# The head of a pre-layernorm transformer layer in another order: early weights, VectorE low halves, second x ahead of the feed-forward's weights, dummy transposes

## What is computed

```python
x = x + attn(layernorm(x))      # causal, ALiBi bias per head, softmax, Wo and bo
x = x + ffn(layernorm(x))       # sigmoid(x1) * x2, weights quantised to -1, 0, 1
# attn: q, k, v = n @ W + b; scores = q k^T / 4 + slope_h * distance; softmax; @ v; @ Wo + bo
# ffn:  w -> clip(round(w / (mean|w| + 1e-8)), -1, 1); hidden = sigmoid(x @ w1.T) * (x @ w2.T); hidden @ w3.T
```

## Time and profile before

| | us |
|---|---|
| median of 3 runs | 677.22 (677.1 to 678.31) |
| the profiled execution, its own time | 679.13 |
| its span on the core | 677.3 |
| PE busy | 617.9 (91%) |
| DVE busy | 463.4 (68%) |
| ACT busy | 366.2 (54%) |
| POOL busy | 118.3 (17%) |
| DMA, moved in all | 57.64 MB, mean 85 GB/s |

### The profile page before, as it was taken

One profiled execution on the slowest core, in us unless ns is written; L12 is line 12 of the kernel. 1 busy time (PEld: TensorE's weight loads), 2 busy tenths in 40 slices (PEclk: granted clock), 3 DMA queues, 4 the chain that ended last, 5 costly groups with the idle time before them and its releaser, 6 DMA issues.

```text
span 677.3 us, 10966 instructions
## 1 busy us (share of the span) xinstructions
PE 617.9 (91%) x3710; PEld 378.2 (56%) x3710; DVE 463.4 (68%) x1189; ACT 366.2 (54%) x770; POOL 118.3 (17%) x146
## 2 busy tenths in 40 slices
PE   1787888889999989999999999899999999999997
PEld 1444555546565646455556575555555555565486
DVE  4357878666776967568787778778788787511075
ACT  2424454564554435647655535467677675576521
POOL 5464300031021220320001212003100000132100
PEclk9959998899999979999999999899999999999999
DMA  8664664555131313543231131136332120011000
GB/s 249 168 176 117 163 145 111 132 171 144 33 80 34 95 32 81 174 128 81 64 69 45 33 88 41 48 80 131 95 97 49 39 76 0 2 42 42 1 17 31
DMA packets 26635, 57.64 MB, mean 85 GB/s; under 512 B 4756, under 2 KB 14484, under 8 KB 22996
## 3 DMA queue, kind: packets, MB, share of 16 engines
q1 hardware_dynamic: 26580, 56.95, 32.8%
HBM read 41.87 MB, written 14.80 MB: 84 GB/s over the span
## 4 chain that ended last, share of the span: by engine, by line
PE 78%; DVE 9%; ACT 4%; issue 4%; DMA 3%; SPq 1%; POOL 0%; ACTq 0%; POOLq 0%
PE pS L940 20%; PE pO L953 19%; PE pM L920 18%; PE pM L895 5%; PE pM L841 3%; PE pM L904 3%; DVE pm L1092 2%; PE pS L943 2%; DVE pM L1095 2%; PE pM L881 2%; PE pS L904 1%; PE pM L847 1%; ACT probs L785 1%; DMA qst<-mT 1%; PE pS L841 1%
## 5 line engine op out<-in xcount | busy, mean ns | idle before, releaser
L785 ACT ACTIVATE probs<-pS 128x512 f32<-128x512 f32 (+3 forms) x640 | 308.5, 545 | 247.0 <-PE pS L943 122.0
L1092 DVE TENSOR_REDUCE pm<-pM 128x1 f32<-128x512 f32 x384 | 240.4, 681 | 64.2 <-PE pM L920 63.2
L920 PE MATMUL pM<-kst,qst 126*128 126x512 f32 (+3 forms) x640 | 240.3, 404 | 22.0 <-ACT qk_hl L742 6.0
L940 PE MATMUL pS<-qst,kst 128*128 128x512 f32 (+3 forms) x640 | 249.7, 406 | 6.6 <-DMA qst<-mT 4.4
L940 PEld LDWEIGHTS pS<-qst,kst 128*128 128x128 f32 x640 | 121.5, 192 | 88.7 <-issue 57.4
L1095 DVE CUSTOM_DVE_ANT_0 pM<-pM,mask 128x128 f32<-128x128 f32 (+3 forms) x256 | 119.3, 517 | 66.0 <-PE pM L920 65.6
L920 PEld LDWEIGHTS pM<-kst,qst 126*128 126x128 f32 x640 | 122.8, 198 | 51.5 <-ACT qk_hl L742 7.0
L953 PE MATMUL pO<-probs,vals 128*17 128x512 f32 (+3 forms) x1280 | 134.9, 540 | 0.0
L953 PEld LDWEIGHTS pO<-probs,vals 128*17 128x17 f32 x1280 | 29.6, 97 | 65.7 <-issue 40.9
L943 PE MATMUL pS<-maskb,identb 128*128 128x128 bf16 x256 | 59.0, 233 | 0.0
L642 POOL TENSOR_TENSOR rstd<-ve,mhalf 128x4 f32<-128x4 f32 (+1 forms) x9 | 8.5, 945 | 219.5 <-DVE ve L1008 219.4
(11 more groups left out here) (145 smaller groups left out, 418.8 us busy)
## 6 DMA issues: line engine op xcount, KB each, us to landing
kst<-parts SPq DMA_DIRECT2D x40, 512.0 KB
parts<-qk_hl SPq DMA_DIRECT2D x32, 256.0 KB, 3.1
qst<-parts SPq DMA_DIRECT2D x32, 256.0 KB, 4.5
ctx_dram<-ctx_raw SPq DMA_DIRECT2D x15, 256.0 KB, 4.0
xin<-in_L_attn_x SPq DMA_DIRECT2D x5, 512.0 KB, 5.4
out<-work SPq DMA_DIRECT2D x8, 256.0 KB, 2.2
work<-ctx_dram SPq DMA_DIRECT2D x7, 256.0 KB
work<-rden_dram SPq DMA_DIRECT2D x7, 256.0 KB
```

Of the source, the lines that this page charges most:

```text
L785: nc.scalar.activation(probs[:, n % PSLOTS, q0:CH], pS[:, n % SBANKS, q0:CH], ACT.Exp)\
L920: pe.matmul(max_bank(x)[:, 0:N], qst[0:R_MAX, u % QSLOTS, h, t * P:(t + 1) * P], kst[0:R_MAX, n % KSLOTS, h, 0:N], start=True, stop=True). ...
L940: ins = pe.matmul(pS[:, n % SBANKS, q0:CH], kst[0:R_END, sl, h, b:b + P], qst[0:R_END, u % QSLOTS, h, q0:CH], start=True, stop=not is_diag ...
L1092: nc.vector.tensor_reduce(dst, bank, AX.X, ALU.max).then_inc(max_free, 1)
```

## The change

- **SP**: Wk and Wq come right behind x of chunk 0 and have a semaphore of their own (`wqk_in`), the biases of k and q too (`bias_in`). Then Wv and bv, x of chunk 1 and the table's parts, and only then w1 and w2. w3 comes behind the stores of k(0,1) and q(0,1), Wo and bo behind `load_q(1)`.
- **PE**: 30 transposes of the identity into itself (`WARM_UP`) run from the moment the identity is there; nobody reads them. The transposes of chunk 0 start tile by tile (`xn0_ok`). k(1,0) and q(1,0) run among the turns of unit 0, after its 4th and its 8th turn; k(1,1) and q(1,1) take their old place after `swap_max(0)`; v(1,0) and v(1,1) are now the groups of steps 0 and 1, and steps 2 and 3 have none.
- **ACT and DVE**: for k(0,0), q(0,0), k(0,1), q(0,1) ACT writes the high half only, and DVE makes the low half straight from PSUM (`split_head`). The factor of q goes into its weights. For all other k and q groups nothing changes, except that ACT applies no factor.
- **POOL**: the constants of the masks come behind the first layernorm, `key_rows(0)` and the zeros of `qst` ahead of it, the ones of `qst` behind it.
- **DVE**: layernorm of chunk 0 is first, the table second; the statistics of chunk 1 stand between `split_head` of q(0,0) and of k(0,1).

The core of the diff:

```diff
-            lst = lst[4:] + [None] * 3
+            lst = lst[6:] + [None] * 5
...
-    head_first, head_last = pre_groups(0) + pre_groups(1)[:2], [("gamma",)] + pre_groups(1)[2:4]
-    head_groups = head_first + head_last
+    head_first, head_last = pre_groups(0) + pre_groups(1)[:2], [("gamma",)] + pre_groups(1)[4:6]
+    head_between = {G - 1: ("k", 1, 0), 2 * G - 1: ("q", 1, 0)}
+    head_groups = head_first + list(head_between.values()) + head_last
+    head_splits = [g for g in head_first if g[0] in "kq"]
+    WARM_UP = 30
...
+        def need_split(eng, g):
+
+            if g in head_splits:
+                need_empty(eng, g)
+            else:
+                eng.wait_ge(split_ok, split_no[g] - len(head_splits) + 1)
...
             load_x(0)
+            for dst, src in ((w_raw[0], Wk), (w_raw[1], Wq)):
+                sp.dma_start(dst, src.rearrange("(k p) n -> p k n", p=P)).then_inc(wqk_in, 16)
             sp.dma_start(al[:, 0, :], alibi).then_inc(al_in, 16)
...
+            sp.dma_start(wv_s[:, :, :], Wv.rearrange("(k p) n -> p k n", p=P)).then_inc(w_in, 16)
+            sp.dma_start(bv_b[:, :], bv.rearrange("(a n) -> a n", a=1).to_broadcast([P, D])).then_inc(w_in, 16)
+            load_x(1)
+            sp.wait_ge(al_ok, 2)
...
-            sp.dma_start(w_rows[2], w3.rearrange("(t p) n -> p t n", p=P)).then_inc(raw_in, 16)
...
             store_parts(("k", 0, 1))
             store_parts(("q", 0, 1))
+            sp.dma_start(w_rows[2], w3.rearrange("(t p) n -> p t n", p=P)).then_inc(w3_in, 16)
             load_k(1)
             load_q(1)
+            sp.dma_start(wo_s[:, :, :], Wo.rearrange("(k p) n -> p k n", p=P)).then_inc(wo_in, 16)
+            sp.dma_start(bo_b[:, :], bo.rearrange("(a n) -> a n", a=1).to_broadcast([P, D])).then_inc(wo_in, 16)
+            store_parts(("k", 1, 0))
+            store_parts(("q", 1, 0))
             load_m(0)
...
+            key_rows(0)
+            query_zeros(0)
+            power(1)
+            pool.wait_ge(xn0_ok, TPC)
+            query_ones(0)
...
+            for g in head_first[:KT]:
+                side_op(g)
+            act.wait_ge(bias_in, 64)
...
+            for g in head_first[KT:KT + len(head_splits)]:
+                side_op(g)
+            act.wait_ge(raw_in, 64)
+            for i in range(2):
+                size_of_weights(i)
+            for g in head_first[-KT:]:
+                side_op(g)
+            for g in head_between.values():
+                side_op(g)
+            act.wait_ge(w3_in, 16)
+            size_of_weights(2)
...
-            pe.wait_ge(const_ok, 1)
-            pe.wait_ge(w_in, 160)
-            pe.wait_ge(w_by_dim, 2)
+            pe.wait_ge(ident_ok, 1)
+            for _ in range(WARM_UP):
+                pe.transpose(pM[:, 0, 0:P], ident[:, :], ident[:, :])
             for g in head_first:
                 side_group(g)
+            pe.wait_ge(const_ok, 1)
             for k in range(n_turns(0)):
                 max_turn(0, k)
+                if k in head_between:
+                    side_group(head_between[k])
...
+            def split_head(g):
+                i = split_no[g]
+                dve.wait_ge(head_hi, i + 1)
+                b = (bias_k if g[0] == "k" else bias_q)[:, g[2]:g[2] + 1]
+                nc.vector.scalar_tensor_tensor(out=qk_hl[:, i % 2, 1, :].bitcast(F32R), in0=bank(g), scalar=b,
+                                               in1=qk_hl[:, i % 2, 0, :], op0=ALU.add, op1=ALU.subtract)\
+                    .then_inc(side_v, 1)
```

More of the change, by code:

```diff
@@ L174, in preln_layer @@
         last[b] = i
-        e = READS_LAST[g[0]]
-        emptied.append((e, 1 + sum(READS_LAST[q[0]] == e for q in order[:i])))
+        e = reads_last(g)
+        emptied.append((e, 1 + sum(reads_last(q) == e for q in order[:i])))
     def ring_groups(groups):
         return [("side", *g) for g in groups if in_s_bank[number[g]] == 0]
-    ring_use = ring_groups(head_first) + [("turn", 0, k) for k in range(n_turns(0))] + [("swap", 0)]
-    ring_use += ring_groups(head_last)
+    ring_use = ring_groups(head_first)
+    for k in range(n_turns(0)):
+        ring_use += [("turn", 0, k)]
+        ring_use += ring_groups([head_between[k]] if k in head_between else [])
+    ring_use += [("swap", 0)] + ring_groups(head_last)
     for s in range(NS):
@@ L318, in preln_layer @@
         rstd_ok = sem("rstd_ok")
+        xn0_ok = sem("xn0_ok")
         xn_ok = sem("xn_ok")
@@ L523, in _ @@
                 sp.dma_start(w_rows[i][0:FH - FF, FT - 1, :], w[FF:FH, :]).then_inc(raw_in, 16)
-            sp.dma_start(w_rows[2], w3.rearrange("(t p) n -> p t n", p=P)).then_inc(raw_in, 16)
-            sp.wait_ge(vself, 2)
-            for part in range(2):
-                sp.dma_start(alibi_parts[part, :, :].rearrange("h (i n) -> (h i) n", n=H * T // P),
-                             al[:, 1 + part, :]).then_inc(al_out, 16)
-            load_x(1)
-            sp.wait_ge(al_out, 32)
             store_parts(("k", 0, 0))
             store_parts(("q", 0, 0))
+            sp.wait_ge(al_out, 32)
             load_k(0)
@@ L681, in split_lo @@
                 nc.gpsimd.tensor_tensor(lo.bitcast(F32R), qk_f[:, :], hi, ALU.subtract).then_inc(split_ok, 1)
-                pool.wait_ge(split_ok, i + 1)
-            key_rows(0)
-            power(1)
-            query_rows(0)
-            split_lo(("k", 0, 0))
-            power(2)
-            split_lo(("q", 0, 0))
-            split_lo(("k", 0, 1))
-            split_lo(("q", 0, 1))
-            for n in range(1, QSLOTS):
+                need_split(pool, g)
+            key_rows(1)
+            power(2)
+            pool.wait_ge(xn_ok, 1)
+            query_zeros(1)
+            query_ones(1)
+            split_lo(("k", 1, 0))
+            split_lo(("q", 1, 0))
+            for n in range(2, QSLOTS):
                 key_rows(n)
-                query_rows(n)
+                query_zeros(n)
+                query_ones(n)
             for g in head_last[1:]:
@@ L792, in save_ctx, with size_of_weights @@
                 nc.scalar.activation(ctx_raw[:, :], pO[:, :], ACT.Copy).then_inc(ctx_saved, 1)
-            act.wait_ge(w_in, 160)
-            for dst, src in ((wk_s, w_raw[0]), (wq_s, w_raw[1])):
-                nc.scalar.activation(dst[:, :, :].rearrange("p k (m d h) -> p (k m) d h", m=KT, d=HD),
-                                     src.rearrange("p k (m h d) -> p (k m) d h", m=KT, d=HD), ACT.Copy)\
-                    .then_inc(w_by_dim, 1)
-            nc.scalar.mul(bias_q[:, :], bq_raw[:, :], HD ** -0.5).then_inc(wsum_ok, 1)
-            act.wait_ge(wsum_ok, 1)
-            for g in head_first:
-                if g[0] != "v":
-                    side_op(g)
-            act.wait_ge(raw_in, 80)
-            for i in range(3):
+            def size_of_weights(i):
                 act.wait_ge(wsum_ok, i + 1)
```

106 lines of the change are left out of this document (71 added, 35 removed).

## The result

| | before | after |
|---|---|---|
| median, same chip | 678.25 us (675.11 to 683.75, 20 runs) | 675.36 us (670.37 to 685.59, 20 runs) |
| ratio | | 0.9954 [0.9934, 0.9974] |
| the profiled execution | 679.13 us, span 677.3 | 673.38 us, span 671.6 |

The kernel is faster by 0.46%, 3.1 us by the ratio (2.9 by the medians). The two profiled executions differ by 5.8 us, which is more; where the other 2.7 us come from is part of what follows.

The account below looks back on a forecast made before the run. PE's pipeline, 78% of the chain, was taken as bound and untouched, so only the head and units 0 and 1 count: first scores 48.1 plus 30.8 put `split_max(2)` at 78.9, 4.1 us earlier, giving 673.1 us; range 668.6 to 676.9.

Parts of the forecast that it names:

- Up to the first turn: Head, from weights to unit 0's first turn: first turn at 29.5 us, between 28.0 and 32, against 35.15.
- k(0,0) at 3.7 us: First projection on PE: stays at 3.7 us; 1.9 instead would bring nothing, its store waiting behind w2 all the same.
- The rule that the sum went by: PE's clock in the head: transposes don't count as activity, so the dummies do nothing and k(0,0) stays at 3.7 us.
- the other branch of the argument: PE's clock in the head: if the dummy transposes do count, the first rival holds, 670.7 us, chance 0.28.
- The turns: Unit 0, first turn to swap: 8.2 us plus 3.8 of stalls, k(1,0) at low clock; swap at 41.5 against 43.4.
- To the first scores: Swap to first scores: 6.6 us, or 8.4 for k(1,1) at the low clock; scores at 48.1 against 49.22.
- Units 0 and 1: First scores to `split_max(2)`: 16.2 us to `split_max(1)`, then 14.6, together 30.8 against 33.8, a gain of 3.0.
- Sum at `split_max(2)`: Head plus units 0 and 1: `split_max(2)` at 78.9 us against 83.0, a gain of 4.1.
- Behind it, unchanged to 1 us: Span behind `split_max(2)`, 594 us: unchanged to 1 us; a change of more than that was a sign of being wrong.
- Rival 1: Clock stays high into the turns: swap at 39.1, scores at 45.7, gain 6.5, 670.7 us; chance 0.28.
- Rival 2: Clock low for all four projections of chunk 1: scores at 52.3, gain 0.0, 677.2 us; chance 0.12.
- Rival 3: DMA queue becomes the bound at `load_m(0)`: m lands at 53.6, slower at 678.6 us; chance 0.10.

Follow-up runs that it names:

- w_late: Changed kernel with w1 and w2 issued behind the stores of k(0,1) and q(0,1), ACT's sums behind chunk 1's transposes; 675.00 us, ratio to before 0.9956.
- warm0: Changed kernel without the 30 dummy transposes (WARM_UP = 0); median 673.57 us, ratio to the kernel before 0.9922.
- ones_beside: Changed kernel with POOL's fill of the ones of qst beside the first layernorm instead of behind it; one execution, first turn at 29.91 us.
- pool_split: Changed kernel with POOL making all low halves as before, none by DVE from PSUM; median 676.86 us, ratio to the kernel before 0.9969.
- weights_last: Changed kernel with Wk and Wq issued behind the other small loads, as before; one execution, first turn at 29.41 us.
- after_again: The changed kernel once more, unchanged, in the last group of runs; median 674.88 us, ratio to the kernel before 0.9949.
- x_back: Changed kernel with x of chunk 1 issued behind w1 and w2, as before; median 675.62 us, ratio to the kernel before 0.9941.
- hold: Changed kernel with more dummy transposes: before chunk 1's transposes and the first turn, among the turns, behind the projections; 674.60 us, ratio to before 0.9925.
- best: w_late with gamma behind k(1,1) and q(1,1), w3 and Wo later still, plus the dummies of hold; 683.09 us, ratio to the kernel before 1.0030.

## Why the prediction was right, and where its steps were not

The forecast was 673.1 us, 4.1 below the kernel before; measured were 3.1 below. That the sum comes out so near is partly luck: at the swap the kernel was 2.3 us earlier than forecast, and from there to `split_max(2)` it lost 4.1 us against it, mostly by falls of the clock that the sum did not have. Point by point:

- **Up to the first turn: right.** Said 29.5, measured 28.11. The queue decides it: the store took 5.86 us from issue to landing, and w_late, without w1 and w2 ahead, reached the turn 2.9 us earlier. The error of 1.4 us begins at k(0,0), which I put at 12.3 and which ran at 10.44: I had the last tile of the layernorm at 10.3 "at the latest" and the dummies' end at 9.8, and they came at 8.75 and 8.82. So it is the dummies, by a hair, that the transposes wait for, and not the layernorm that was to hide them.
- **k(0,0) at 3.7 us: wrong, and worth nothing, as said.** It took 1.98, because the dummies do raise the clock. That it "brings nothing" is what warm0 shows, to 0.02 us. The rule that the sum went by (transposes don't count) failed here, but the other branch of the argument, that the clock would then stay high into the turns, failed too: it fell all the same before k(1,0) (0.50 from 28 to 32 us), with the eight transposes of chunk 1 in between.
- **The turns: right.** Low clock for k(1,0) (3.31 us), high for q(1,0) (1.88); from first turn to swap I said 12.0 us and it was 11.1.
- **To the first scores: mis-sized.** I said 6.6 us, with k(1,1) at the high clock, and named 8.4 for the low one. It was 8.2: the clock had fallen again during the last turns, and k(1,1) took 3.32. The scores came at 47.45 all the same, 0.65 before the 48.1, since the turn was early.
- **Units 0 and 1: the step that failed.** The term "a gain of 3.0" measured 0.5 (33.3 us against 33.8). I had counted every group by its time at the high clock, since the clock was 1.00 through both units before. The first part should take 16.2 us. In ones_beside, pool_split and weights_last, whose steps of units 0 and 1 are those of the changed kernel, it takes 15.8 (below); in the changed kernel, after_again, warm0, x_back, w_late and hold it is 17.4 to 17.7, and in best 19.7 at a clock of 0.77. The windows of ones_beside, then of after_again, from first scores to `split_max(1)` and on to `split_max(2)`:

```profile
49.69:65.47 15.78, 13.32 (x81) 8.80 (x81) 12.70 (x47) 5.90 (x13) 9.01 (x5) 1.00 0.25 76
65.47:80.68 15.21, 12.35 (x87) 7.58 (x86) 13.38 (x39) 7.25 (x19) 0.00 (x0) 0.89 0.72 160
```

```profile
47.51:64.98 17.47, 15.00 (x81) 10.04 (x81) 12.70 (x46) 5.91 (x13) 9.03 (x5) 0.90 0.18 57
64.98:80.19 15.21, 12.36 (x87) 7.26 (x86) 13.24 (x40) 7.25 (x19) 0.00 (x0) 0.89 0.72 160
```

  The same 81 matmuls and the same work on DVE, at a clock of 1.00 and of 0.90: the counting of stalls was right to 0.4 us, and what was missing is a fall of the clock that costs 1.7 and that six of the ten executions with these steps had (best had a deeper one). In after it falls on v(1,0), in after_again on v(1,1) (3.68 us). The second part takes 15.2 to 15.65 in all ten, at 0.89, where I had 14.6. What in the order brings the clock down there wasn't found.
- **Sum at `split_max(2)`:** said 78.9, measured 80.73 and, in after_again, 80.19. So 2.3 to 2.8 us of gain, not 4.1. The timed gain of 3.1 us, with an interval of 1.8 to 4.5, fits this and can't tell it from 4.1.
- **Behind it, unchanged to 1 us: right of the work, wrong of the time.** The instructions and the busy times of DVE and ACT are the same, but 594.3 us became 590.9. In after_again, the same program, it is 594.4 us again, so the 3.4 us aren't the change's doing. By the sign that the prediction named (a change of more than 1 us there), the first profile spoke against it; with this scatter, the sign was too sharp for one execution.
- **The rivals.** Rival 1 (clock high into the turns) happened where the dummies of hold forced it (hold and best), and for k(1,0) in weights_last. Rival 2 had half of its case: two of four projections low. Rival 3 didn't happen: the wait of the first scores in the changed kernel ended with ACT's half of q(1,1), not with `load_m(0)`.

**Where the rest of the time between executions lies.** I took the time from one `split_max` to the next in all 14 profiled executions. From unit 4 to 5 it is 33.4 to 33.5 us in twelve of them and 31.9 in two (after, warm0). From unit 7 to 8 it is 38.5 us in twelve and 41.5 in two (before, weights_last). Others, like 6 to 7 (33.1) or 13 to 14 (45.4 to 45.5), are the same in all. The windows of the stretch behind `split_max(4)` show what the step of 1.5 us is, first the kernel before, then the one after:

```profile
122.00:126.00 4.00, 4.00 (x27) 2.20 (x26) 2.45 (x4) 1.92 (x4) 0.00 (x0) 0.58 0.94 215
```

```profile
116.10:124.00 7.90, 5.59 (x45) 4.13 (x44) 5.85 (x12) 4.53 (x11) 0.00 (x0) 1.00 0.62 133
```

The clock fell to 0.58 in one and stayed at 1.00 in the other. From unit 7 to 8 it is 0.92 in before and weights_last, and 1.00 in after. So of the 5.8 us between the two profiled executions, 2.1 had been won by `split_max(4)`, 1.5 come between units 4 and 5 and 3.0 between units 7 and 8, less 0.8 in the next. The 1.5 and the 3.0 are falls of the clock that one execution had and the other not; the 0.8 isn't, for the clock is 1.00 in both there. Over the timed runs that the ratios count and whose clock is on record, the time goes with the mean granted clock: 77 runs of the kernel before have a slope of -5.6 us for 0.01 of clock (correlation -0.88), 30 of the changed kernel -3.8 (-0.85). At an equal clock of 0.978 the two lines stand at 679.0 and 674.7 us, 4.3 apart; the changed kernel's mean clock is 0.9763 against 0.9786. That it pays back a part of its gain through a lower clock is what these numbers suggest, but don't show: for the 20 runs of the kernel before that were timed beside the first 20 of the changed one, no clock is on record. What makes the clock fall in one execution and not in another wasn't found.

**Which part is worth what** stays open in one respect. Undone alone, the dummies, the order of x and DVE's low halves each cost the first turn nothing (within 0.2 us), the early weights 1.3 and the place of POOL's fill 1.8. That is 3.1 of the 7.0 us, each read from one execution. The parts may cover each other, so that undoing one alone understates it; they weren't tried in pairs. The place of the ALiBi table behind the layernorm, and the split of the single semaphore for ten loads, were not undone at all.

## What to carry to other kernels

Read how long a store takes to land when other loads stand ahead of it in the queue: 1.44 MB ahead cost 2.9 us at the first turn, and a faster projection, split or warm clock in front of such a store was worth nothing here. A stretch of thin work has two lengths or more, one with TensorE's clock high throughout and others with a fall in it (15.8 us at a granted clock of 1.00, 17.5 at 0.90 here); price both, and look at a mark 50 to 100 us further on before believing an early one. Where the gain sought is half a per cent, one profiled execution can't carry it: two of the same program differed by 3.0 us, half of it in one step of 1.5.

## What the hardware showed that was not expected

**Transposes raised the clock.** Thirty fp32 transposes of 128x128 ran from 2.45 to 8.82 us, with nothing else on PE, and k(0,0) at 10.44 takes 1.98 us; without them 3.78.

**A fill on POOL stopped some operations of DVE from SBUF to SBUF for its whole length, and others not at all.** The clearest rows of the first kind are small operations on 128x3 elements behind `split_max(0)` in the changed kernel, DVE first, then POOL:

```profile
40.17 0.14 DVE L1227 TENSOR_SCALAR thr<-pM 128x3 f32<-128x3 f32 x1
40.34 1.66 DVE L1228 TENSOR_SCALAR thr<-thr 128x3 f32<-128x3 f32 x1
42.04 1.82 DVE L1229 TENSOR_SCALAR thr<-thr 128x3 f32<-128x3 f32 x1
```

```profile
40.18 1.80 POOL L670 MEMSET qst<- 62x2048 f32 x1
42.03 1.80 POOL L674 MEMSET qst<- 2x2048 f32 x1
```

The one that reads PSUM takes 0.14 us beside the fill. The next two, with source and destination in SBUF, end when the fills end (41.98 and 43.83). DVE's turns, which read PSUM, keep their 0.33 to 0.73 us in the kernel before, where fills lie beside them from 39.80 to 43.46. The Trainium skill, "SBUF — State Buffer", section "SBUF: two separate sides", describes, for those operations of DVE that use the pair of ports that it shares with GpSimd, an exclusive lock that the second to come waits for through the whole instruction, and not shared bandwidth; these rows, and the 1.38, 2.94 and 4.50 us of the normalisation with none, one and two fills beside it, agree.

Not every operation from SBUF to SBUF is held. In the changed kernel the layernorm's four `BATCH_NORM_STATS2` (L1064) take 1.41 us from 4.13 on, beside a fill from 4.32 to 6.12, and as much in the kernel before. The `TENSOR_TENSOR` on 128x256 elements (L1202) takes 0.43 us at 8.98, inside the fill from 8.87 to 10.69, and in the kernel before the `TENSOR_REDUCE` of L1104 takes 0.18 us at 43.05, inside the fill that ends at 43.46. Even a `TENSOR_SCALAR`, on 128x4 elements (L1071), takes 0.17 us at 5.98, inside the fill that ends at 6.12. Held were, in these rows, the `TENSOR_SCALAR` of the normalisation and the two of `thr`; no run here shows what sets them apart.
